# Where a maximum unit stands among the matmuls of a score block

## The reference

```
scores = jnp.einsum('bknh,bqnh->bnqk', keys, queries) / jnp.sqrt(jnp.asarray(H, scores_dtype(residual)))
causal_mask = q_idx < k_idx
scores = jnp.where(causal_mask[None, None, :, :], jnp.asarray(EPS, scores.dtype), scores)
probs = jax.nn.softmax(scores, axis=3)
weighted = jnp.einsum('bnqk,bknh->bqnh', probs, values)
```

## Time and profile before

| | us |
|---|---|
| median of 3 runs | 2626.65 |
| lowest and highest | 2624.95, 2632.76 |
| profiled execution | 2634.17 |
| its span in the profile | 2632.4 |

### The profile page before, as it was taken

How to read it: one execution, slowest core, us unless ns; L and a number is a source line. 1 busy time by engine, 2 the same in 40 slices (tenths; PEclk the granted TensorE clock), 3 DMA queues, 4 the chain that set the end, 5 groups by cost and what they waited for, 6 DMA issues and landing times. The chain is left out here.

```text
span 2632.4 us, 30363 instructions
## 1 busy us (share of the span) xinstructions
PE 2308.0 (88%) x9988; PEld 1193.7 (45%) x10080; DVE 1496.2 (57%) x3862; ACT 825.9 (31%) x1173; POOL 1254.2 (48%) x1141
## 2 busy tenths in 40 slices
PE   4479999999999999999999999999999936878777
PEld 2224444444444444444444444444444415566565
DVE  3575656666575757565656656574757522433534
ACT  1113433334343333433333334333333410110101
POOL 0006574747474756556574747474756821101010
PEclk8659999999999999999999999999999967888998
DMA  4554344453535364635344353535353224021120
GB/s 132 151 120 107 98 119 118 102 142 96 140 87 136 81 157 114 150 79 143 98 119 119 102 144 99 135 87 137 80 149 85 62 82 162 16 80 56 40 96 16
DMA packets 208476, 278.64 MB, mean 106 GB/s; under 512 B 69264, under 2 KB 87888, under 8 KB 208336
## 3 DMA queue, kind: packets, MB, share of 16 engines
q1 hardware_dynamic: 208336, 276.91, 39.7%
HBM read 181.93 MB, written 94.63 MB: 105 GB/s over the span
## 5 line engine op out<-in xcount | busy, mean ns | idle before, releaser
L687 POOL TENSOR_TENSOR acc<-acc,probs 128x512 f32<-128x512 f32 (+1 forms) x960 | 1064.4, 1143 | 428.4 <-ACT probs L907 428.3
L907 ACT ACTIVATE probs<-ps_s 128x1024 f32<-128x1024 f32 (+2 forms) x640 | 552.8, 898 | 410.3 <-PE ps_s L772 227.7
L770 PE MATMUL ps_s<-qq,kk 128*128 128x512 f32 (+3 forms) x1280 | 639.2, 500 | 33.7 <-ACT probs L907 33.7
L956 DVE TENSOR_REDUCE partial<-ps_bg 128x1 f32<-128x512 f32 x768 | 513.4, 687 | 198.2 <-PE ps_bg L718 128.7
L791 PE MATMUL ps_o<-probs,v 128*64 128x512 f32 (+3 forms) x2560 | 539.5, 542 | 20.4 <-DVE num L990 18.0
L772 PE MATMUL ps_s<-qm,kl 128*128 128x512 f32 (+3 forms) x1280 | 469.0, 366 | 0.0
L718 PE MATMUL ps_bg<-k_bf,q_pad 128*128 128x512 bf16 (+3 forms) x1188 | 405.3, 363 | 56.3 <-DVE partial L953 18.0
L705 PE MATMUL ps_bg<-xs,w_in 128*128 128x512 f32 x768 | 365.1, 600 | 21.5 <-DMA xs<-xn_turned 19.0
L770 PEld LDWEIGHTS ps_s<-qq,kk 128*128 128x128 f32 x1280 | 247.8, 194 | 196.3 <-issue 119.9
L680 POOL TENSOR_TENSOR acc<-probs 128x512 f32<-128x512 f32 x96 | 120.6, 1277 | 417.4 <-ACT probs L907 417.4
L953 DVE CUSTOM_DVE_ANT_0 junk<-ps_bg,mask_q 128x512 bf16<-128x512 f32 (+3 forms) x512 | 242.3, 486 | 100.0 <-issue 94.0
(11 more groups left out here) (102 smaller groups left out, 1708.2 us busy)
## 6 DMA issues: line engine op xcount, KB each, us to landing
high_and_low<-split SPq DMA_DIRECT2D x128, 512.0 KB, 5.5
qq<-high_and_low SPq DMA_DIRECT2D x64, 512.0 KB, 4.6
kk<-high_and_low SPq DMA_DIRECT2D x128, 256.0 KB, 5.4
c_o_in<-heads_turned SPq DMA_DIRECT2D x10, 2048.0 KB, 8.1
qm<-high_and_low SPq DMA_DIRECT2D x64, 256.0 KB, 6.3
kl<-high_and_low SPq DMA_DIRECT2D x64, 256.0 KB, 6.7
e<-masked_weights SPq DMA_DIRECT2D x128, 128.0 KB, 2.9
scale<-inverse_sums SPq DMA_DIRECT2D x128, 128.0 KB, 2.8
```

Source lines behind the costliest of these rows:

```text
L687: g.tensor_tensor(acc[h][:, group % 2, q0:q0 + w], acc[h][:, group % 2, q0:q0 + w], probs[h][:, probs_slot(i, t), at:at + w], ALU.add).the ...
L770: pe.matmul(out, kk[:, h, kb * P:(kb + 1) * P], qq[:, h, q], start=True, stop=False, skip_group_check=True)
L907: nc.scalar.activation(probs[h][:, probs_slot(i, t), 0:width], ps_s[:, h, 0:width], ACT.Exp, scale=SCORE_SCALE).then_inc(p_ready, 1)
L956: e.reduce_max(to, ps_bg[:, n % 2, 0:w], AX.X).then_inc(max_read, 1)
```

## The change

For a slot with a score block, the maximum unit moves from behind the block to between its two products. For the two slots with weighted() it stays behind the products. The unit itself, its wait, the number of units, DVE's order and ACT's order are as they were. The diff:

```
-                def scores(t, h, n):
+                def scores(i, t, h, n, slot):
...
                     pe.matmul(out, kk[:, h, kb * P:(kb + 1) * P], qq[:, h, q], start=True, stop=False,
                               skip_group_check=True)
+                    maxima(i, slot)
                     mm = pe.matmul(out, kl[:, h, kb * P:(kb + 1) * P], qm[:, h, q], start=False,
                                    stop=not diagonal, skip_group_check=True)
...
+                def maxima(i, n):
+
+                    for u in range(NMAX):
+                        if MAX_AT[u] == n and i + 1 < N:
+                            max_unit(i + 1, u)
+
                 def between(i, n):
...
-                    for u in range(NMAX):
-                        if MAX_AT[u] == n and i + 1 < N:
-                            max_unit(i + 1, u)
...
-                        scores(0, h, n)
+                        scores(0, 0, h, n, -1)
...
                                 if ni < N:
-                                    scores(nt, h, n)
+                                    scores(i, nt, h, n, 6 * t + 2 * h + n)
                                 between(i, 6 * t + 2 * h + n)
                         for n in range(2):
                             weighted(i, t, n)
+                            maxima(i, 6 * t + 4 + n)
                             between(i, 6 * t + 4 + n)
```

## The result

| | us |
|---|---|
| before, median of 6 runs | 2627.28 (2624.8 to 2632.76) |
| after, median of 6 runs | 2692.11 (2683.37 to 2695.45) |
| ratio, 95% interval | 1.024 (1.0222 to 1.0258) |
| profiled executions, before and after | 2634.17 and 2692.4 |

The account below looks back on a forecast made before the run. PE was taken as the bound, busy 117.83 of 123.40 us a pair. Junctions 2.59 plus mask steps 0.45 gave 3.04 us a pair; 15 x 3.04 = 45.6 on 2626.65 gave 2672 us, range 2654 to 2688.

Parts of the forecast that it names:

- the mechanism: At a pass's start the first unit stays 1.17 us behind slot 5's first; the score product formerly ahead now runs after.
- eleven junctions: Starts of unit passes within a pair, where the first block's second score product was to be lost: 2.59 us a pair.
- First term, the junctions: At starts of unit passes, PE loses the first block's second score product, plus any mask product: 2.59 us a pair.
- Inside a pass: nothing: Between two units of a pass the score products take 0.47 us either way, so mid-pass units lose nothing.
- absorption at the end: In a pair's last two unit passes, a 0.58 us wait for DVE swallows the earlier pass's loss, leaving 0.24 us.
- Second term, the mask steps: In wide diagonal tiles, each mask product followed by a score product costs 0.05 us more: 9 x 0.05 = 0.45 a pair.
- Score ready later: ACT's exponentials start up to 0.23 us later against PE, more behind a stall; cover about 2.2 us, so cost 0.
- the rest was taken as fixed: Stages outside the 15 pairs with units: no change allowed for; the pairs' 45.6 us was simply added to 2626.65.
- the theory's: In the follow-up runs: the loss arises where a pass starts, after the two units of slot 5; 0.2 to 0.3 us each.

## Why the prediction was wrong in size

The direction was right, and so was the mechanism in most passes; the time, 2672, was 20 us short of the measured median and 10 us short of the repeated one. Two things were put too low: the pair (3.04 forecast, 3.52 measured, 7 us in all), and what lies outside the pairs, which the sum put at nothing (12 us in the first comparison). The first alone would have left the time inside the range, at 2626.65 + 52.8 = 2679.5.

By kinds of passes, forecast and measured in us a pair: plain 1.37 and 1.34; the first two wide diagonal ones 0.90 and 0.99; the first two narrow ones 0.38 and 0.35; the last two with units 0.39 and 0.73; the two at the ends, 6 and 19, nothing and 0.08. The prediction says eleven junctions and lists twelve; the thirteenth, into pass 19, it leaves out.

**First term, the junctions.** For passes 7, 9 and 10 the mechanism was the one forecast: with only slot 0 moved they lose 0.21 to 0.24, and without the double unit next to nothing. Pass 14 loses its 0.23 with either part of the positions moved. In passes 8 and 13 the number was right by luck. "Inside a pass: nothing" was wrong there: DVE's chain holds a unit in mid-pass, that wait swallows the junction's loss, and the B behind the held unit costs the same 0.23. Narrow diagonal passes: 0.19 forecast, 0.16 to 0.19 measured, but of these 0.10 to 0.13 go with the place of the mask product, for which no more than 0.07 was forecast.

**The step that failed in the pair: absorption at the end.** I wrote that DVE works without a gap from 1043.14 to 1046.39, so that the wait in the earlier trace rows swallows the loss of the pass before, and took 0.24 for the two. They lost 0.56 and 0.17. The chain has a gap, too small to be listed as idle. In the changed kernel it is wide enough:

```profile
1075.08 0.34 DVE L1007 RECIPROCAL inverse<-total 32x32 f32<-32x32 f32 x1
1075.65 0.45 PE L718 MATMUL ps_bg<-k_bf,q_pad 128*128 128x128 bf16 x2
...
1075.93 0.29 DVE L958 CUSTOM_DVE_ANT_0 junk<-ps_bg,mask_q 128x128 bf16<-128x128 f32 x1 [0.51 <-issue]
```

DVE is free at 1075.42 and starts the read 0.28 us behind the unit's issue. In the kernel before (its repeat) the same two stand 0.28 apart as well:

```profile
1054.10 0.34 DVE L1002 RECIPROCAL inverse<-total 32x32 f32<-32x32 f32 x1
1054.23 0.45 PE L718 MATMUL ps_bg<-k_bf,q_pad 128*128 128x128 bf16 x2
...
1054.51 0.29 DVE L953 CUSTOM_DVE_ANT_0 junk<-ps_bg,mask_q 128x128 bf16<-128x128 f32 x1
```

There DVE was free at 1054.44 and the read began 0.07 later: it was PE that set it. So PE's delay went straight through. With the mask steps 0.39 us had been forecast for the two and 0.73 came: 0.34 us a pair, some 5 in all.

**Second term, the mask steps.** 0.05 a step from two ends was a little small; the run with the mask first gives 0.07, and 0.02 x 9 steps in 15 pairs are 3 us in all. The term's range (0 to 0.14) held it.

**Score ready later: right.** PE's waits for ACT are 2.1 us in both.

**The step that failed outside the pairs: the rest was taken as fixed.** 15 x 3.52 = 52.8 us explain the repeated comparison (51.8) and leave 12 us of the first. I added the loss to one median of three runs and gave nothing for the stages outside the pairs, although the profiled execution was already 7.5 us off that median. The profiles show where the rest varies. In the twelve profiles of kernels with these stages unchanged the first L747 stands between 313 and 327 us (the two with short reads apart; up to 3.5 us of it are the first pair's own loss). It follows the moment at which the clock rises to stay full, 192.6 to 205.1 us: from there to the mark it is 120.6 to 121.7 us in all twelve, once the first pair's own loss or gain is taken off. And the sixteenth pair, without units, lasts 92 or 99 us. Why the clock rises earlier or later stays open, and so does how much of the 12 us each of the two made, since only one execution of a comparison has a profile.

The Trainium skill (TensorE: Matmul & The Clock Gate, "Wait — 56ns, not 53.3ns?") gives 215.7 ns for 512 columns, by which a plain junction would have been an estimated 0.22 us. The passes lost 0.20 to 0.23, so these runs do not tell it from the 0.23 of the rows.

## What to carry to other kernels

With two buffers between a fast producer and a slower reader, count what the producer does between a fill and the one after the next, and compare it with issue to release. Moving work from ahead of a fill to behind it costs nothing where the fill does not wait, and its full length once behind the last fill of a stretch that does; what was lost at an earlier fill is then swallowed. So look for every fill that is held, not only for the one where the count falls. Before letting a later wait swallow a delay, look also whether the reader's start is set by itself or by the producer: a gap of 0.07 us decides it. And where the parts of a sum can be measured, compare the parts: twice here the sum was met by other passes than the theory's.

## What the hardware showed that I had not expected

- A unit between the two halves of the value products (64 output columns each) costs 0.25 us beyond its own time, 2.35 against 2.10, though a unit between two full-width products costs only its 0.23.
- With DVE free, its read of a 512-wide bf16 product began 0.43 us behind the issue (983.82 to 984.25), of a 128-wide one 0.28 (1054.23 to 1054.51). Cutting the read from 0.69 to 0.23 us therefore cuts issue to release by less than half.
- DVE operations that take 0.75 us can take far longer: L985 38.42 us in the last pair, until 0.55 us after POOL's additions pause, and the same operation 1.53 us in every pair of one run with another order on PE. By the times they wait for POOL; no run tests it.
- The pair's time repeats to 0.02 us between runs of one kernel (123.35 and 123.37; 126.87 and 126.89), while the whole repeats to 10 us. For a change inside the pairs the profile is the finer measure by far.
